# Attention kernel on eight cores: five query-key score chunks no longer issued together at the start of each query block

## What is computed

```
xn = layernorm(x)
Q, K, V = xn @ Wq, xn @ Wk, xn @ Wv          # 16 heads of 64
alpha = softmax(Q K^T / 8)                   # over ALL 4096 keys
alpha = where(causal, alpha, 0)              # the mask comes AFTER the softmax
s = alpha V
g = silu(ffn(xn))                            # routed attention with one head of 128
out = x + s * g
```

## Time and profile before

| | |
|---|---|
| median of 3 runs | 3853.19 us (3843.02 to 3905.13) |
| the profiled execution | 3848.39 us |
| span of its cores, first to last instruction | 3837.1 to 3846.8 us |
| mean granted TensorE clock of the cores | 0.776 to 0.780 |
| P3 on core 0, first exponential to the end of the last item | from 1156.2 to about 3672 us |

### The profile page before, as it was taken

How to read it: one execution, slowest core, us unless ns; L and a number is a source line. 1 busy time by engine, 2 the same in 40 slices (tenths; PEclk the granted TensorE clock), 3 DMA queues, 4 the chain that set the end, 5 groups by cost and what they waited for, 6 DMA issues and landing times.

```text
span 3846.8 us, 60418 instructions; the slowest of 8 cores (3837.1 to 3846.8 us)
## 1 busy us (share of the span) xinstructions
PE 2578.9 (67%) x18642; PEld 1156.7 (30%) x18642; DVE 2313.8 (60%) x6185; ACT 2169.6 (56%) x2500; POOL 254.4 (7%) x706
## 2 busy tenths in 40 slices
PE   0312999766747877777777777777777777777700
PEld 0201444333323333333333333333333333333300
DVE  3527777404335676667667667666766766777733
ACT  3000000261107688679669778867966977899910
POOL 0020000000000000001001000000100100010021
PEclk9996999888977767776876786787687678676655
DMA  6540000001130000000000000000000000000078
GB/s 180 170 131 1 1 1 1 1 15 71 69 110 3 2 5 5 4 4 7 2 4 5 5 2 5 5 4 4 7 2 4 5 5 3 5 6 5 6 227 300
DMA packets 40390, 133.94 MB, mean 35 GB/s; under 512 B 6290, under 2 KB 6290, under 8 KB 40082
## 3 DMA queue, kind: packets, MB, share of 16 engines
q1 hardware_dynamic: 27346, 88.12, 7.3%
q0 software_dynamic: 12736, 41.95, 3.8%
HBM read 96.50 MB, written 33.55 MB: 34 GB/s over the span
## 4 chain that ended last, share of the span: by engine, by line
PE 29%; ACT 23%; DVE 19%; issue 15%; DMA 10%; DVEq 3%; POOL 0%; ACTq 0%; SPq 0%; POOLq 0%
ACT stagef L1314 7%; ACT expC L1299 7%; PE PB L853 6%; DMA stagef<-x 5%; PE PB L838 4%; DVE cacc L1053 4%; ACT R L1314 4%; PE PB L767 3%; PE PB L770 3%; ACT stagef L1299 3%; DVE tmpc L1170 3%; PE PB L867 3%; PE PB L726 3%; PE PB L782 3%; DMA s_stage<-s_sp 2%
## 5 line engine op out<-in xcount | busy, mean ns | idle before, releaser
L1170 DVE TENSOR_REDUCE tmpc<-stagef 128x2 f32<-128x1024 bf16 (+2 forms) x726 | 809.8, 1126 | 318.1 <-ACT stagef L1314 271.7
L1299 ACT ACTIVATE expC<-PB 128x1024 bf16<-128x1024 f32 x768 | 835.2, 1097 | 118.1 <-PE PB L853 117.2
L1314 ACT ACTIVATE stagef<-PB 128x1024 bf16<-128x1024 f32 x600 | 658.7, 1099 | 188.0 <-PE PB L867 155.6
L1170 DVE TENSOR_REDUCE tmpc<-R 128x2 f32<-128x1024 bf16 (+2 forms) x362 | 406.0, 1121 | 155.1 <-ACT R L1314 134.1
L1299 ACT ACTIVATE stagef<-PB 128x1024 bf16<-128x1024 f32 x384 | 420.0, 1094 | 72.0 <-PE PB L853 71.2
L654 PE MATMUL PB<-R,xnT 128*128 128x512 bf16 x1536 | 340.3, 381 | 74.4 <-DVE qk_tmp L1053 72.9
L853 PE MATMUL PB<-R 64*128 64x512 bf16 x1152 | 290.2, 493 | 142.0 <-ACT stagef L1314 79.9
L853 PE MATMUL PB<-QTt,KTt 64*128 64x512 bf16 x1152 | 286.9, 487 | 139.6 <-ACT stagef L1314 77.2
L1314 ACT ACTIVATE R<-PB 128x1024 bf16<-128x1024 f32 x296 | 325.8, 1101 | 78.0 <-PE PB L867 60.1
L867 PE MATMUL PB<-R 64*128 64x512 bf16 (+3 forms) x1088 | 255.7, 460 | 99.9 <-ACT expC L1299 31.9
L867 PE MATMUL PB<-KTt,QTt 64*128 64x512 bf16 (+3 forms) x1088 | 252.8, 454 | 101.5 <-ACT expC L1299 33.2
(11 more groups left out here) (167 smaller groups left out, 2971.3 us busy)
## 6 DMA issues: line engine op xcount, KB each, us to landing
stagef<-x SPq DMA_DIRECT2D x96, 512.0 KB, 4.8
out<-stagef SPq DMA_DIRECT2D x32, 512.0 KB, 4.2
g_sp<-stagef SPq DMA_DIRECT2D x32, 256.0 KB, 2.0
s_sp<-s_stage POOLq DMA_DIRECT2D x64, 128.0 KB, 2.4
expC<-g_sp POOLq DMA_DIRECT2D x32, 256.0 KB, 6.5
R<-qp POOLq DMA_DIRECT2D x8, 512.0 KB, 5.2
R<-kp POOLq DMA_DIRECT2D x8, 512.0 KB, 4.8
R<-vp POOLq DMA_DIRECT2D x8, 512.0 KB, 4.9
```

Of the source, the lines that this page charges most:

```text
L1170: e.tensor_reduce(s.tmpc[:].rearrange("p (h c) -> p h c", h=2)[:, :, c:c + 1], s.c1scr((m1 - 1) % 3)[:, 0:2 * kw] .rearrange("p (h k) -> p ...
L1299: e.activation(s.expCs(es), PB[[0, 1, 3][it["slot"]]][:, :], AF.Exp).then_inc(sem["aC2"], 1)
L1314: e.activation(scr[:, 0:1024], pbsrc[:, 0:1024], AF.Exp).then_inc(sem["aC1"], 1)
```

## The change

Two lines of `p3_sched` are removed. The rest of the file is the same.

```diff
@@ -67,8 +67,6 @@
                 c1p += 1
         sched.append(("C2", (j, t)))
         target = min(C1_NIT, math.ceil((k + 1) * C1_NIT / len(c2l)))
-        if t == 1 and j <= 6:
-            target = min(C1_NIT, max(target, c1p + 5))
         while c1p < target:
             sched.append(("C1", C1_ITEMS[c1p]))
             c1p += 1
```

## The result

| | before | after |
|---|---|---|
| median | 3847.19 us (10 runs) | 3753.07 us (10 runs) |
| ratio, 95% interval | | 0.9758 [0.9733, 0.9783] |
| the same kernel in a later comparison | | 3733.05 us, 0.9692 [0.9645, 0.9738] |
| profiled execution, slowest core | 3846.8 us | 3764.9 us (core 7) |
| profiled execution, core 0 | 3846.8 us | 3736.5 us |

The change makes the kernel faster by 2.4% in the first comparison and by 3.1% in the second; 2.8% was forecast. In some executions of most kernels here TensorE's granted clock is lower on a pair of cores or on several, and the time some per cent longer; the ratios leave these out, e4_after_8scratch is read on its undisturbed core 4, and e5_scratch_and_two in its repetition e5b_scratch_and_two. Lines after the removed ones stand two lower in the file: L853, L867, L1170 and L838 of before are L851, L865, L1168 and L836 now.

What follows compares the result with a forecast made beforehand. P3 was taken as bound by ScalarE's stream of exponentials with holes; 101 us in pairs 0 to 6 plus 11.2 in pair 7 less 4.4 in block 0 gave 108, so 3745 us, range 3710 to 3790.

Steps and rivals of the forecast that it cites:

- The bound: P3 is ScalarE's stream of exponentials with holes; all 108 us of gain there would reach the end.
- The burst: Starts of blocks 6 to 1: losses behind C2 (j,1) fall to 2.7 us in pairs 0 to 6, 4.1 in pair 7.
- The step by which 0.6 of 1.53 us stays: Block start: the C1 waiting for VectorE's scratch gets its turn one item later, so 0.6 us of 1.53 stay lost.
- TensorE's wait for the evacuation: Each block's first product would wait 0.5 to 0.9 us; ScalarE could go on 0.2 us before VectorE frees the scratch.
- The pairs: P3: a head pair goes from 321 to 307 us, the last one from 260 to 250.
- Block 0: One exponential instead of two covers the mask's wait: 0.55 us lost per pair, 4.4 in all; bounds gain 0.9, loss 1.2.
- The QKVb items: Holes behind QKVb in blocks 6, 5, 4 become 3.2, 3.7 and 3.7 us, leaving 10.6 a pair.
- some 8 us a pair: By the skill's clock rule alone, the three QKVb items start at full clock: 16 us less over seven pairs.
- The clock rival: P3: half clock more often slows projection matmuls, giving back 60 us, total 3805 us; chance 0.07.
- A wrong sign to look for: P3: ScalarE's waits for VectorE's sums fall from 68.6 us to 20 to 35.
- The total: Whole kernel: median 3745 us, 2.8% less.

Runs made afterwards that it cites:

- e4_after_8scratch: Changed kernel with eight C1 scratch buffers instead of three: ratio 0.9706 [0.9597, 0.9814], P3 2397.4 us on core 4.
- e5_scratch_and_two: Changed kernel with eight scratch buffers and at least two C1 items behind C2 (j,1), five in block 0: ratio 0.9686 [0.9612, 0.9761].
- e5b_scratch_and_two: Repetition of the changed kernel with eight scratch buffers and at least two C1 items behind C2 (j,1): ratio 0.9706 [0.968, 0.9732], P3 2395.5 us on core 0.
- e3: Kernel before, its order kept, with eight C1 scratch buffers instead of three: P3 2429.4 us, ratio 0.9775 [0.9709, 0.9841].
- e1: Kernel before with its rule of five C1 items kept only for blocks 6, 5 and 4: P3 2476.7 us, ratio 0.9911 [0.9876, 0.9946].
- a2_after_again: Changed kernel run once more, unaltered, against the kernel before: P3 2398.2 us on core 0, ratio interval 0.9645 to 0.9738.
- e7: Kernel before with the three QKVb items moved behind C2 (6,8), (5,8) and (4,8): P3 2467.9 us, ratio 0.9879 [0.9819, 0.9939].
- b1: Changed kernel with the three QKVb items moved behind C2 (6,8), (5,8) and (4,8): P3 2374.8 us, median 3709.07 us, ratio 0.9647 [0.9626, 0.9668].
- b2: Changed kernel with eight scratch buffers, two C1 items behind C2 (j,1), all left in block 0, QKVb items moved: P3 2355.4 us, ratio 0.965 [0.9603, 0.9698].

## Why the prediction was right, point by point

**The bound.** That P3 is ScalarE's stream with holes, and that each hole closed reaches the end, held to the microsecond: 110.6 us less in P3, 110.3 us less on core 0.

**The burst.** Forecast for the starts of the blocks 6 to 1: 23.0 us left (2.7 in each of seven pairs, 4.1 in the last). Measured: 25.6. The step by which 0.6 of 1.53 us stays is in the rows above as 0.64. Experiment e3 shows the cause apart from the order, and e1 that the blocks add up.

**TensorE's wait for the evacuation** appears with 0.86 us in the row above and 45.5 us in 55 waits over P3, and doesn't reach ScalarE as long as the scratch is later. It is closer behind than I said (e4).

**The pairs** went to 307.8 us (307 forecast) and the last to 251.0 (250), and the QKVb in block 4 has its copy 0.11 us behind its matmuls, as said.

**Block 0** was the one term that was mis-sized by more than half: forecast a loss of 4.4 us, measured 7.0, inside the bounds given. I had let the last C1's scores start at 1796.75, 0.57 us behind the first masked product; they start 0.58 behind it in the new rows as well. But this product now starts 3.72 us behind the exponential of C2 (0,1) (1754.40 to 1758.12), and in the earlier trace rows it starts 3.34 behind it (1792.84 to 1796.18): the spill is issued 2.25 us behind that exponential and not 1.87. The evacuation of block 1 comes later by these 0.38 us against ScalarE's stream, which I had taken as fixed. TensorE's rows show what delays it, first before and then after: the score matmuls of C2 (0,1), behind which the last product of block 1 stands.

```profile
1791.30 0.39 PE L853 MATMUL PB<-R 64*128 64x512 bf16 x2 [0.52 <-ACT stagef L1314]
```

```profile
1752.97 0.61 PE L851 MATMUL PB<-R 64*128 64x512 bf16 x2 [0.29 <-ACT stagef L1312]
```

They took 0.39 us at a granted clock of 1.00, and take 0.61 at 0.50. They also start 1.43 us ahead of the exponential of C2 (0,1) and not 1.54, which makes 0.1 us of the 0.38; the rest goes with the clock. In the changed kernel they take 0.61 in all eight pairs. In the kernel before they did so in pairs 2, 4 and 7 alone, where block 0 lost 1.5 us already and not the 1.21 of pair 1, from which I had worked. In the second profile of the changed kernel (a2_after_again) pair 7 has 0.39 as well, and its block 0 lost 1.98 us and not 2.20. Why the clock is at its lower level at this place in nearly every pair stays open.

**The QKVb items**: forecast 3.2, 3.7 and 3.7 us in blocks 6, 5 and 4, measured 3.1, 3.5 and 3.9 on the mean of seven pairs. That a C1 sum ahead of the copy sets the hole in block 5 is borne out where its matmuls are fast. Which of them stands at which clock I left open, and there lay what more could be had: e7 and b1 show 6.8 and 7.2 us a pair when all or most of them run at full clock, and the changed kernel has 10.5. The Trainium skill ("TensorE: Matmul & The Clock Gate", What's actually happening) has the slow clock as the resting state that activity releases; by it alone, with the burst's hole gone, I had worked out some 8 us a pair, which is about 56 in seven pairs. The measured 73.3 are against that reading: the item of block 4 in all pairs and that of block 6 in four of seven still ran mostly at half clock although no hole of the old size stood ahead of them. Where b1 has these two they find it full.

**The clock rival** did not come: the granted clock in a pair is 0.74 against 0.73 and in the last one 0.67 against 0.68; QKV items that didn't move cost 313.9 us, 2.8 less than before. A part of what it describes is seen at one place, in block 0 as told above, and in e4 and e5b, where the block starts were closed further.

**A wrong sign to look for.** I said that ScalarE's waits for VectorE would fall from 68.6 to 20 to 35 us. They fell to 10.2:

```profile
ACT stagef L1312 <- DVE tmpc L1168: 5.1, 17, 0.5
ACT R L1312 <- DVE tmpc L1168: 3.4, 9, 0.9
ACT stagef L1315 <- DVE tmpc L1168: 1.2, 5, 0.2
ACT R L1315 <- DVE tmpc L1168: 0.5, 2, 0.2
```

The time was right and the sign was read on the wrong scale. A wait in this view begins at the recorded end of the exponential before it, and that lies up to 0.4 us behind the next start at pace (lengths of 1.30 for starts 0.905 apart). Each wait is smaller by this than the time that is lost. In the earlier trace rows 1.16 us stand for a loss of 1.53, and here 0.24 for 0.64.

**The total** was forecast at 3745 us and is 3753 in one comparison and 3733 in the other. In the profiled execution of the first, the clock of cores 6 and 7 in P1, which the prediction took as that of the profile before, is what put the slowest core behind; that it makes all of the difference between the comparisons is not shown. A little of the closeness is chance: the gain at the block starts and behind the three QKVb items was 115.0 us where the prediction's terms make 112, the other QKV items gave 2.8 that it didn't have, and block 0 took back 2.6 more than it said.

## What to carry to other kernels

Where one engine's stream has a steady pace, lay the list of work beside its starts, subtract the pace, and add up the holes by their place: the sum forecast P3 to 3 us in 2509 here. A bunch of one kind of work put in front of a wait doesn't hide the wait if the same slow engine must also clear the buffers of that bunch; by turns, one item of the other kind pays for most of it. And a burst's backlog is met by whatever stands behind it, so move large items away from it, and look at which clock they run.

## What the runs showed of the hardware

- Eight matmuls of 512 columns took 1.89 us or 3.54 to 3.57 us, by the level of the clock. Behind C2 (6,8) it was the fast one in kernels with and without a run of C2 items (e7, b1; in one pair of e7 they took 2.17 us). Behind C2 (6,5) it was the slow one in four pairs of seven, but the fast one in all seven with eight scratch buffers (e4, core 4). So the place alone doesn't settle it. I had not expected a move by some items to be worth 23 us (b1), or 41 where it also leaves the backlog (e7).
- Holes closed at the block starts and in block 0 (24 us) came back by 19 us behind the projections on core 0, at a granted clock of 0.74 instead of 0.76, and nearly whole on most other cores (e5b). In b2, with three QKVb items moved as well, few of them did: 367.3 us of holes there against 363.0 in b1.
- Two neighbouring cores of one execution went through P1 at a mean of 0.81 of the clock, where others had 0.88, and came 31 to 46 us later to P3, with the same instructions as the others. The granted clock held at 0.81 for a whole 100 us of it, while another core had 1.00.
- The same score matmuls of C2 (0,1) took 0.39 us at a granted clock of 1.00 and 0.61 at 0.50. The kernel before shows both at this place, by the pair; the changed kernel shows the second in all eight pairs of its first profile and in seven of its second.
